# Two transformer layers over eight images on one core: splitting queries and keys after the turn instead of before it

## The reference

```
layer 0:  h = LN(x);  windows of 14x14 (padded), q,k turned by the rotary table
          attn = softmax(q*s . k) v   over 12 heads of 16, within the window
          x = x + gamma1 * (attn @ w_proj + b)
          x = x + gamma2 * (gelu(LN(x) @ w_fc1 + b) @ w_fc2 + b)
layer 1:  the same with q not turned, no gammas, and scores
          q*s . k + rel_h[q, k_row] + rel_w[q, k_col]
          where rel_h, rel_w = q . rel_pos_h/w[q_pos - k_pos + 13]
```

## Time and profile before

| | us |
|---|---|
| median of 3 runs | 572.3 |
| lowest, highest | 570.03, 575.05 |
| the profiled execution | 571.97 |
| its span, first to last instruction | 569.8 |

### The profile page before, as it was taken

The page is one execution under the profiler, slowest core; times in us unless marked ns, Lnnn a source line. Parts: engine busy times, 40 slices in busy tenths (PEclk is TensorE's granted clock), DMA queues, the critical chain, the costliest instruction groups (busy, mean ns, idle before and its releaser), DMA issues.

```text
span 569.8 us, 13552 instructions
## 1 busy us (share of the span) xinstructions
PE 521.0 (91%) x4832; PEld 467.3 (82%) x4832; DVE 386.6 (68%) x915; ACT 367.7 (65%) x778; POOL 226.7 (40%) x324
## 2 busy tenths in 40 slices
PE   8767979999899999999999999999999999979875
PEld 7756868799798988888979898888889898868664
DVE  3887699968987758866758678776858677351230
ACT  0442347653959485969687886969688787755501
POOL 8233427625418353334536253343627234030210
PEclk9896699998999999999999999999999999988899
DMA  7410005000000000000000000000000000000000
GB/s 193 115 41 1 3 2 148 2 1 2 3 1 3 2 2 2 3 2 2 2 3 2 12 22 24 4 1 16 4 3 15 1 17 3 16 3 24 6 14 14
DMA packets 11055, 10.44 MB, mean 18 GB/s; under 512 B 3664, under 2 KB 9456, under 8 KB 10992
## 3 DMA queue, kind: packets, MB, share of 16 engines
q1 hardware_dynamic: 9264, 6.79, 4.5%
q10 hardware_dynamic: 1728, 2.81, 1.7%
HBM read 7.75 MB, written 1.57 MB: 16 GB/s over the span
## 4 chain that ended last, share of the span: by engine, by line
PE 57%; issue 17%; DVE 10%; POOL 7%; ACT 5%; DMA 2%; ACTq 0%; DVEq 0%; POOLq 0%
PE ps L1121 15%; PE ps L1324 9%; PE ps L1179 7%; PE ps L1193 5%; PE ps L1246 4%; PE ps L1269 4%; PE ps L1301 3%; DMA QT<-mT 2%; PE ps L1163 2%; PE ps L1219 1%; DVE mneg L713 1%; PE ps L1281 1%; PE ps L1208 1%; POOL QT L1041 1%; POOL xnm L353 1%
## 5 line engine op out<-in xcount | busy, mean ns | idle before, releaser
L882 ACT ACTIVATE PT<-ps 98x392 f32<-98x392 f32 x192 | 94.4, 496 | 52.7 <-PE ps L1246 51.6
L713 DVE TENSOR_REDUCE mneg<-ps 98x2 f32<-98x392 f32 x192 | 106.6, 560 | 32.1 <-PE ps L1193 29.9
L1246 PE MATMUL ps<-QT,KM 128*98 128x196 f32 x384 | 80.7, 293 | 3.1 <-DMA QT<-mT 2.4
L1193 PE MATMUL ps<-KM,QT 128*98 128x196 f32 x384 | 78.2, 286 | 3.6 <-DVE mneg L713 3.2
L1121 PE MATMUL ps<-WQ,XHa 128*128 128x384 f32 (+2 forms) x320 | 64.3, 305 | 5.4 <-DVE XHa L610 3.2
L1324 PE MATMUL ps<-W,GT 128*128 128x192 f32 x384 | 65.8, 328 | 2.6 <-ACT GT L924 2.5
L1121 PE MATMUL ps<-XHm,WF 128*128 128x256 f32 x384 | 64.6, 288 | 1.1 <-DVE XHm L610 1.0
L964 POOL TENSOR_SCALAR vepsm<-mvm 128x2 f32<-128x2 f32 x16 | 3.1, 193 | 155.8 <-DVE mvm L589 155.8
L1324 PEld LDWEIGHTS ps<-W,GT 128*128 128x128 f32 x384 | 62.0, 190 | 3.6 <-ACT GT L924 3.6
L812 ACT ACTIVATE KM<-ps 64x512 fp32r<-64x512 f32 x80 | 47.4, 592 | 24.7 <-PE ps L1179 24.2
L1193 PEld LDWEIGHTS ps<-KM,QT 128*98 128x98 f32 x384 | 52.2, 169 | 11.4 <-issue 4.0
(11 more groups left out here) (162 smaller groups left out, 1149.8 us busy)
## 6 DMA issues: line engine op xcount, KB each, us to landing
X<-in_x SPq DMA_DIRECT2D x8, 94.5 KB
out<-X SPq DMA_DIRECT2D x8, 94.5 KB
W<-in_w ACTq DMA_DIRECT2D x1, 576.0 KB, 5.6
W<-in_w SPq DMA_DIRECT2D x1, 576.0 KB, 3.9
raw<-in_w ACTq DMA_DIRECT2D x1, 384.0 KB, 3.5
raw<-in_w ACTq DMA_DIRECT2D x2, 192.0 KB, 4.2
raw<-in_w SPq DMA_DIRECT2D x1, 384.0 KB, 4.2
raw<-in_w SPq DMA_DIRECT2D x2, 192.0 KB, 4.8
```

The lines of the kernel that those rows point to most:

```text
L713: v.tensor_reduce(mneg[n % 2][0:CH, 0:2 * NH].rearrange("p (t h) -> p t h", t=2)[:, :, h], bank[0:CH, 0:2 * NM].rearrange("p (t k) -> p t ...
L882: a.activation(PT[:, at % (2 * GROUP), :], ps[0:CH, ST_BANK + h % 2, 0:2 * NM], ACT.Exp)\
L1193: last = mm(ps[0:CH, S_BANK + h % 2, NM * t:NM * t + NM], QT[p][:, h, CH * t:CH * t + CH], KM[p][:, h, 0:NM], start=True, stop=True)
L1246: last = mm(ps[0:CH, ST_BANK + h % 2, NM * c:NM * c + NM], KM[p][:, h, CH * c:CH * c + CH], QT[p][:, h, 0:NM], start=True, stop=True)
```

## The change

The features of q and k are reordered on the host so that within a half of six heads the dimension is outer and the head inner (`by_dim`): partition d*6 + h after a transpose. q and k are transposed as plain features, 96 of them at a time (qf and kf, four transposes each, in both layers), split there into high (ScalarE) and low (VectorE) parts in a new tile SPL, and put into the rows of QT and KM by DMAs from SyncE: three for the keys and three for the queries of each half, each 96 partitions x 1 KB to 16 partitions x 6 heads x 1 KB. From slot 2 on a fourth one per half writes zeros into row 52. In layer 1 only the relative terms are still stacked (RS, 64 columns a head) and transposed (r0 to r2). Rows 48 to 63 are written once, by four DMAs. The loads of images 3 to 7, the second layer's weights and the stores get ticks of their own, and all tables are new.

```
-        {"k0": KQ_DVE, "k1": KQ_ACT, "k2": KQ_ACT, "q0": KQ_DVE, "q1": KQ_DVE, "q2": KQ_ACT},
...
+ROWS_ENGINE = {"r0": TO_ACT, "r1": TO_ACT, "r2": TO_DVE}
+HF = NH // 2
...
+        first = sb("first", [128, 2 * 1024], F32R)
+        RS = first[:, 0:2 * NH * 64].rearrange("p (t h d) -> p t h d", t=2, h=NH)
+        SPL = [sb(f"SPL{p}", [HP, 4, 2, NT], F32R) for p in range(2)]
...
-        SCORES = -58
+        SCORES = -59
...
+            {"et1": 25, "h2": 104, "qk0": -113, "o1": 62, "es1": -30, "qk1": -113, "ve": -86, "h0": 102,
+             "o0": 61, "mx": 95, "dn": 108, "h1": 103, "es0": -49, "m": -9, "pr": 77, "x": -126, "qf": -75,
+             "on": 69, "kf": -80, "v01": -98, "et0": 10},
+            {"g0": -102, "h1": 103, "kf": -111, "qf": -111, "m": -9, "g1": -101, "on": 71, "dn": 109, "mx": 95,
+             "g3": -96, "h2": 103, "es0": -27, "x": -127, "o1": 59, "pr": 78, "et0": 3, "o0": 56, "ve": -87,
+             "r1": -68, "h0": 101, "v01": -94, "r2": -50, "g2": -100, "et1": 18, "qk0": -118, "es1": -26,
+             "qk1": -118, "r0": -70},
...
+             "gelu0": 100, "gelu1": 101, "gelu2": 102, "pk0": -84, "pq0": -72, "pk1": -54, "pq1": -58,
+             "row": -20},
...
+             "gelu0": 100, "gelu1": 101, "gelu2": 103, "rh0": -88, "rh1": -78, "rl0": -70, "rl1": -68,
+             "pk0": -99, "pq0": -86, "pk1": -65, "pq1": -56, "row": -20, "store": 108},
...
+                 "qkv1": 152, "clear": 194, "img3": -122, "img4": -50, "img5": -27, "img6": 0, "img7": 52,
+                 "w1": 61, "wp1": 403, "w21": 441}
+        MOVES = {("prepare", 1): -10, ("mlp", 14): 18, ("prepare", 3): 4, ("prepare", 6): 2, ("prepare", 7): 2,
...
+        def all_placed(n, f):
+            return placed[n % 2][f], 16 * (6 + 7 * (n // 2))
...
+        def relative_rows(u, n, copy, eng, done):
+
+            p, j = n % 2, int(u[1])
+            last_head = 4 * j + 3
+            eng.wait_ge(e.stmm, NH * (n - 2) + last_head + 1)
+            eng.wait_ge(e.etmm, 2 * (n - 2) + (1 if last_head < PAIRS else 2))
+            eng.wait_ge(e.rT, 3 * (n - B) + ROWS.index(u) + 1)
             bank = misc(u, n).rearrange("p (m t) -> p m t", m=2)
...
+            copy(QT[p][64:128, 4 * j:4 * j + 3:2, :], bank[0:64])
+            copy(QT[p][64:128, 4 * j + 1:4 * j + 4:2, :], bank[64:128]).then_inc(done, 1)
...
+            def constant_rows():
+                sp.wait_ge(S.cleared, 1)
+                sp.wait_ge(S.pads, 1)
+                for p in range(2):
+                    for tile, k in ((QT[p], 0), (KM[p], 1)):
+                        sp.dma_start(tile[48:64, :, 0:NT].bitcast(F32),
+                                     pads[48:64, k:k + 1, :].bitcast(F32).broadcast_to([16, NH, NT]))\
+                            .then_inc(pads_in, 16)
+
+            def place(n, f, keys):
+
+                p = n % 2
+                tile = KM[p] if keys else QT[p]
+                if n == 0:
+                    sp.wait_ge(S.cleared, 1)
+                if n >= 2:
+                    sp.wait_ge(e.stmm, NH * (n - 2) + HF * (f + 1))
+                    sp.wait_ge(e.etmm, 2 * (n - 2) + f + 1)
+                sp.wait_ge(e.kl if keys else e.ql, n + 1)
+                for part, row in ((2, 0), (2, 16), (3, 32)) if keys else ((0, 0), (0, 32), (1, 16)):
+                    sp.dma_start(tile[row:row + HD, HF * f:HF * f + HF, 0:NT].bitcast(F32),
+                                 SPL[p][:, part, f, :].bitcast(F32)).then_inc(placed[p][f], 16)
+                if n >= 2 and not keys:
+                    sp.dma_start(QT[p][MAX_ROW:MAX_ROW + 1, HF * f:HF * f + HF, :].bitcast(F32),
+                                 mTt[NH + HF * f:NH + HF * f + HF, :].bitcast(F32)).then_inc(placed[p][f], 16)
...
+            def low_parts(n, keys):
+
+                part, high, low = (2, e.kh, e.kl) if keys else (0, e.qh, e.ql)
+                dve.wait_ge(high, n + 1)
+                bank = misc("kf" if keys else "qf", n)[0:HP, :].rearrange("p (f t) -> p f t", f=2)
+                v.tensor_tensor(SPL[n % 2][:, part + 1], bank, SPL[n % 2][:, part].bitcast(F32), ALU.subtract)\
+                    .then_inc(low, 1)
...
+            def high_parts(n, keys):
+
+                part, done, high = (2, e.kT, e.kh) if keys else (0, e.qT, e.qh)
+                act.wait_ge(done, n + 1)
+                bank = misc("kf" if keys else "qf", n)[0:HP, :].rearrange("p (f t) -> p f t", f=2)
+                if not keys and n >= B:
+                    queries_T(n, bank)
+                if n >= 2:
+                    for f in range(2):
+                        act.wait_ge(*all_placed(n - 2, f))
+                copy(SPL[n % 2][:, part], bank).then_inc(high, 1)
...
+            def transpose_heads(n, keys):
+                l = layer(n)
+                if l == 0:
+                    pe.wait_ge(e.qkr, n + 1)
+                else:
+                    pe.wait_ge(e.qk, 2 * n + 2)
+                u = "kf" if keys else "qf"
+                wait_misc_free(pe, u, n)
+                bank, src = misc(u, n), QKa if l == 0 else QK
                 for f in range(2):
                     for t in range(2):
...
+                        at = C * keys + HP * f
+                        last = T(bank[0:HP, NT * f + 128 * t:NT * f + 128 * t + 128], src[:, t, at:at + HP], ident[:])
+                last.then_inc(e.kT if keys else e.qT, 1)
...
+                    pe.wait_ge(pads_in, 4 * 16)
+                if h % HF == 0:
+                    pe.wait_ge(*all_placed(n, h // HF))
+                if layer(n) and h % 4 == 0:
+                    pe.wait_ge(*misc_emptied(f"r{h // 4}", n))
```

380 lines of the change are left out of this document (165 added, 215 removed), and 16 rows, old and new, of tables (USES, WORK).

## The result

**526.7 us** (median of 4 runs, 522.7 to 528.8) against 573.5 us of the kernel before on the same chip (570.0 to 575.1); ratio 0.918, 95% interval 0.911 to 0.926. The forecast was 544, its range 531 to 562: right in sign, and 17 us short. The profiled execution took 528.8 us, its span is 527.0 (569.8 before). Where one execution of a version was over 1.5% slower than its fastest, at a lower granted clock, the median has it and the ratio does not (the run with ScalarE's load alone and the very last one).

The account below looks back on a forecast made before the run. TensorE's work was taken to bound the period from about the third to the fourteenth image. 572.0 + 1.7 (start) - 25.6 (transposes) + 1 (VectorE waits) - 2 (row of maxima) - 3 (end) = 544.1, forecast 544 us, range 531 to 562.

Parts of the forecast that it names:

- The unit of four transposes: TensorE, middle images: 288 transposes fewer, 0.40 us a unit over 6 layer-0 and 8 layer-1 images, 25.6 us gained.
- The stalls between: Layer 1: copies lie beside TensorE; +1 us for waits that a fuller VectorE makes, between 0 and 8.
- The row of maxima: TensorE's weight loads wait less for this row, as its transposes move from -7 to -9: -2 us, 0 to -4.
- The end: Last-but-one perceptron moves behind the last image's projection and covers TensorE's waits: -3 us, from 0 to -4.
- The start: First score at 38.2 us in place of 36.5, after copies, issues and landing: +1.7 us, between -5 and +6.
- The placements: SyncE's on-chip DMAs into QT and KM: issues near 0.74 us, latency hidden within 17 ticks; counted 0.
- the first rival: Placements set the period, overtaking TensorE in layer 0 at 0.90 us an issue; slower from about 1.15; chance 0.12.
- No score that waits for more than 0.5 us: Sign that the forecast holds: no score waits longer than this for a DMA into QT or KM.
- signs of being wrong: Placements at 0.9 us and more, scores waiting on them, or TensorE's busy share under 95% in the middle.
- VectorE takes over: Rival: VectorE, 86% busy in layer 1, holds score maxima back; layer 1 keeps 32 us, total 560; chance 0.11.
- A unit is worth its busy time: Rival: each unit of four transposes is worth 0.63 us, gaining 40.3 in place of 25.6, total 529; chance 0.07.

Follow-up runs that it names:

- the run with ScalarE's load alone: Kernel after the change, with eight small ScalarE copies added ahead of each of the two high-part copies of an image: 539.7 us, ratio 0.941 to before.
- the very last one: Kernel after, with late constants and image 3 loaded behind the first placements, W2 two ticks later, second relative-rows unit one tick earlier: 522.1 us, 0.911 to before.
- the repeats: Kernel after the change, with 288 transposes put back by repeating those of its existing units, nothing else moved: 546.2 us, ratio 0.953 to before.

## Why the prediction was short

Against the profiled execution (528.8 for a forecast of 544.1) 15.3 us are to be explained. By the table above, from image 0 to 15 the work fell by 33.0 us, where I had 25.6, and the stalls by 6.7, where my terms made it 1: 7.4 and 5.7 us. The end gave 1.7 more than forecast, the start 0.2, and what stands around the span 0.4. Even my lower bounds, all added (-5 for the start, -4 for the row, -4 for the end, nothing for VectorE, and 25.6 for the transposes), give 533.4, which is still above the 528.8.

- **The unit of four transposes: mis-sized.** I took 0.40, "the distance by which the next work moves up", and 64 units; it is 0.43 to 0.44 and 72 units, 31.1 in place of 25.6. The distance from the first load of a unit to the first load of the next work leaves out a piece: a score product behind a transpose starts 28 ns after it, but its own pair is then 172 ns apart in place of 91, so a part of the last transpose stands in the product's spacing. By starts of matmuls, transposes are 108 to 110 ns apart. The first two images count too, in part: with the repeats put back, image 0's first transposed score comes 2.2 us later (61.8 and 64.0) for 32 more transposes, 3.5 us at full price. This is the number that the Trainium skill gives (TensorE: Matmul & The Clock Gate, "LDWEIGHTS (loading the stationary operand)", P / 1.2 ns) for 128 columns. Its rule is not thereby shown: it has 80 ns for 96 columns, and the transposes of line 1178 with 96 columns are 108 to 110 ns apart as well.
- **The stalls between: put at +1 where they fell, the step that failed.** I wrote of the copies "All this lies beside TensorE: I count +1", and of GpSimd's subtractions nothing. They did lie beside it by busy share, and still stood in its way by their chains: 13.0 us of idle time in front of the transposes, 8.2 of them behind image 0's first transposed score. In the traces stalls between image 0 and 13 fall by 7.1 us, where my terms made it 1. The experiments say that even this understates it: with all transposes put back, the kernel after is 26.8 us faster than before and has 20.4 us less of stalls, and the transposes are worth 5.3 us in the old order and 19.5 in the new (15 and 24 by the spans, with the clock's part as estimated above taken out). My way of adding prices, each at the place of before, can't give that.
- **The row of maxima, -2:** nothing was gained (4.6 to 4.4 us).
- **The end, -3:** the stretch became 4.7 us shorter, 5.7 by stalls. The move that I counted is worth 1.5 in before, and all three moves of the end 1.2 in after; the rest comes with the freer engines or the rest of the order, and isn't separated.
- **The start, +1.7:** the first score came 5.4 us later, as I had let "the constant rows ... before the turn ends" cost nothing and had not put image 3's six issues (3.9 us) in front of the placements. By the first transposed score 1.5 us of it were left.
- **The placements, 0:** not quite. They do not set the period, and their issue takes 0.597 us, less than my 0.74; the first rival's 0.90 isn't near. The section of the Trainium skill named there treats GpSimd's path and not SyncE's queue; what was drawn from it, that an issue of 96 pieces costs like one of 12, agrees with the runs all the same. "No score that waits for more than 0.5 us" was wrong for the rows of zeros (six waits, 8.2 us in all, one of them behind W2) and for the start, so one of my signs of being wrong, scores that wait on placements, did show.
- **VectorE takes over:** no. It is busy 126.6 of 145.1 us between images 8 and 13, 87% (forecast 86%), and TensorE waits there for 0.32 us a slot. The low parts took 0.684 us (0.69).
- **A unit is worth its busy time (0.63):** no; the time came out near that rival's 529 for another reason.

What stays open: how much of the 26.8 us is the relief of ScalarE and GpSimd and the fewer turns, and how much an order that a fresh search could have found for the old work. Taking the loads of ScalarE and GpSimd away in before gives 11.5 us of it besides the transposes (16.8 - 5.3); VectorE's copies in layer 0 were not taken away, a fresh order for before was not tried, and no run holds the clock fixed.

## What to carry to other kernels

Read the idle column in front of the very instructions that a change removes or frees: an engine at 98% whose groups sit idle for chains of other engines (13 us here, 8 of them past the start) gains twice when those chains go with the work. With in-order queues and a few rotating buffers an instruction has no price of its own: the same 288 transposes were worth 5 us in one order and 19 in another, and a unit moved by two ticks cost 15 us. Part of such a difference can be the granted clock, so compare it before stalls are blamed for all. And where two engines are named for one wait, shorten one and look: here the matmul's line named VectorE, and it was GpSimd. Take work out, write the order anew for what is left, and expect from the first without the second little; to price a unit, double it and look at the distance.

## What was not expected of the hardware

- A DMA of 96 pieces within the chip holds its queue's engine for 0.597 us, one row of 12 pieces for 0.79: the issue does not grow with the pieces. But constant rows broadcast while other transfers run took 0.60 to 2.20 us each to issue.
- The first score product behind a transpose is recorded 28 ns after it, and the next follows after 172 ns in place of 91: the distance over one unit reads 0.40 us, the difference between one and two units 0.44.
- A score product behind a transposed score is followed by the next after 90 ns, one behind weighted values after 171 ns: where a product stands among others moves up to 0.08 us between them, and the sum of a slot's work stays (30.44 and 30.31 us for 301 matmuls in two quite different orders).
